# Making the rows of the maxima on ScalarE and GpSimd instead of VectorE in an attention block

## The reference, cut to what matters

```python
q, k, v = split(x @ W_qkv.T)            # 16 heads of 8
q, k = rope(q), rope(k)
scores = where(causal, q @ k.T / sqrt(8), -inf)
out = softmax(scores) @ v
x = layernorm(x + out @ W_o.T)
x = layernorm(x + x @ quantised(kernel) + bias + (x @ a) @ b)
```

## Time and profile before

| | |
|---|---|
| median of 3 runs | 443.64 us (441.98 to 443.79) |
| the profiled execution | 442.17 us, span 440.4 us |
| TensorE busy | 415.8 us, 94% |
| TensorE weight loads | 205.3 us, 47% |
| VectorE busy | 379.3 us, 86% |
| ScalarE busy | 317.4 us, 72% |
| GpSimd busy | 119.3 us, 27% |

### The profile page before, as it was taken

The page is one execution under the profiler, slowest core; times in us unless marked ns, Lnnn a source line. Parts: engine busy times, 40 slices in busy tenths (PEclk is TensorE's granted clock), DMA queues, the critical chain, the costliest instruction groups (busy, mean ns, idle before and its releaser), DMA issues.

```text
span 440.4 us, 8586 instructions
## 1 busy us (share of the span) xinstructions
PE 415.8 (94%) x3246; PEld 205.3 (47%) x3246; DVE 379.3 (86%) x491; ACT 317.4 (72%) x643; POOL 119.3 (27%) x188
## 2 busy tenths in 40 slices
PE   5989899799999999999999999999999999999982
PEld 2546445344436353455443644444354454435651
DVE  2878799899999999999999999999987988585585
ACT  2454884386975687777888788878788878898760
POOL 8979602102113100223110322011003012225463
PEclk9999999799999999999999999999999999999996
DMA  7522322210000000022200022200000000000001
GB/s 241 177 97 90 111 81 71 56 30 3 2 0 2 4 1 3 1 80 63 61 3 0 2 66 77 60 3 0 2 1 2 1 3 2 3 25 2 1 26 48
DMA packets 12201, 16.58 MB, mean 38 GB/s; under 512 B 2444, under 2 KB 7324, under 8 KB 12160
## 3 DMA queue, kind: packets, MB, share of 16 engines
q1 hardware_dynamic: 11072, 15.75, 11.3%
q0 software_dynamic: 1088, 0.28, 0.4%
HBM read 10.37 MB, written 5.24 MB: 35 GB/s over the span
## 4 chain that ended last, share of the span: by engine, by line
PE 81%; DVE 8%; ACT 5%; issue 3%; POOL 1%; DMA 1%; POOLq 0%; DVEq 0%; ACTq 0%
PE ps L1289 28%; PE ps L1275 23%; PE ps L1231 17%; DVE pmax L1052 7%; ACT probs L974 4%; PE ps L1199 3%; PE ps L1298 2%; PE ps L1245 1%; PE ps L1241 1%; PE ps L1205 1%; PE ps L1255 1%; PE ps L1317 1%; POOL rstd L856 1%; PE ps L1215 1%; DMA wqkv_sb<-in_L_attn_W_qkv_dram 1%
## 5 line engine op out<-in xcount | busy, mean ns | idle before, releaser
L1052 DVE TENSOR_REDUCE pmax<-ps 128x2 f32<-128x1024 f32 (+3 forms) x273 | 319.2, 1216 | 34.5 <-PE ps L1231 18.7
L974 ACT ACTIVATE probs<-ps 128x512 f32<-128x512 f32 (+2 forms) x576 | 285.4, 583 | 78.1 <-PE ps L1275 76.6
L1275 PE MATMUL ps<-qS,kS 64*128 64x512 f32 (+3 forms) x664 | 163.8, 404 | 2.7 <-DVE pmax L1052 1.3
L1231 PE MATMUL ps<-kS,qS 64*128 64x512 f32 (+3 forms) x640 | 141.9, 414 | 5.5 <-DVE pmax L1052 2.4
L1289 PE MATMUL ps<-probs,vP 128*9 128x512 f32 (+3 forms) x1328 | 144.3, 520 | 0.2
L1275 PEld LDWEIGHTS ps<-qS,kS 64*128 64x128 f32 x664 | 84.5, 186 | 85.5 <-ACT probs L974 61.4
L1231 PEld LDWEIGHTS ps<-kS,qS 64*128 64x128 f32 x640 | 67.1, 185 | 59.8 <-DVE pmax L1052 28.6
L881 POOL TENSOR_SCALAR_AFFINE_SELECT probs<-probs 128x512 f32<-128x512 f32 x64 | 40.3, 635 | 109.7 <-ACT probs L974 109.6
L890 POOL DMA_DIRECT2D qS<-mrows x34 | 19.6, 578 | 167.6 <-DVE mrows L1072 167.4
L1289 PEld LDWEIGHTS ps<-probs,vP 128*9 128x9 f32 x1328 | 22.2, 89 | 42.2 <-issue 24.4
L1245 PEld LDWEIGHTS ps<-causal_x,ident_x 64*128 64x128 f32 x188 | 19.1, 186 | 0.0
(11 more groups left out here) (116 smaller groups left out, 196.1 us busy)
## 6 DMA issues: line engine op xcount, KB each, us to landing
qS<-q_parts SPq DMA_DIRECT2D x52, 64.0 KB
kS<-k_parts SPq DMA_DIRECT2D x52, 64.0 KB
cs<-rope_tables_dram SPq DMA_DIRECT2D x4, 512.0 KB, 6.5
q_parts<-qp SPq DMA_DIRECT2D x4, 512.0 KB, 2.9
k_parts<-kp SPq DMA_DIRECT2D x4, 512.0 KB, 2.8
x_sb<-in_L_attn_x_dram SPq DMA_DIRECT2D x4, 256.0 KB, 5.7
out_dram<-rot SPq DMA_DIRECT2D x2, 256.0 KB, 2.3
qS<-mrows POOLq DMA_DIRECT2D x30, 8.0 KB, 1.8
```

The source lines that it names most:

```text
L974: nc.scalar.activation(probs[:, J % PRING, heads[0]:heads[-1] + 1:2, lo:hi], bank_of(("S", n, j, i))[:, 0:len(heads) * (hi - lo)].rearrang ...
L1052: nc.vector.tensor_reduce(dst, src, AX.X, ALU.max).then_inc(unit_free, 1)
L1231: last = nc.tensor.matmul(ps[:, HELD[e][hl], at:at + w], qS[rows, b, c, hp, ii * TOK:(ii + 1) * TOK], kS[rows, b, kk, hp, 0:w], start=i == ...
L1275: last = nc.tensor.matmul(bank_of(("S", n, j, i))[:, x * w:(x + 1) * w], kS[rows, b, j // TPC, hp, (j % TPC) * TOK:(j % TPC + 1) * TOK], q ...
```

## The change

ScalarE copies the transposed maxima as they are from the bank into a new buffer in SBUF, `mraw` (16 rows, 2 buffers of 256), and signals `rows_copied`, which now frees the bank. GpSimd waits for that, makes both parts out of `mraw` and then issues both DMAs as before, at the same place of its order. VectorE's function `rows` is gone. The planner's cost for `M` changes with it: 0.2 us on ScalarE, 0.6 us on GpSimd after a 0.2 us hand-over, nothing on VectorE, and `LANDING` counts from GpSimd. The whole order is planned again with that.

```diff
--- before.py
+++ after.py
@@ -353,8 +353,11 @@
                 self.give(self.act + self.TO_PE, self.sums)
                 self.due += ((self.act + self.TO_PE, "O", n),)
         elif kind == "M":
-            self.aside(0.25, 0.6, ready)
-            self.ready = self.ready[:e[0]] + (self.dve + self.LANDING,) + self.ready[e[0] + 1:]
+            self.act = max(self.act, self.whole(0.25, ready) + self.TO_ACT) + 0.2
+            self.side = (self.side[0] + 0.25, self.side[1])
+            self.give(self.act + self.TO_PE, self.took)
+            self.pool = max(self.pool, self.act + 0.2) + 0.6
+            self.ready = self.ready[:e[0]] + (self.pool + self.LANDING,) + self.ready[e[0] + 1:]
         elif kind == "O":
             g, c, first, end = TASKS[e[0]]
             self.aside(0.55 * (end - first) / TPC, 0.6, ready)
@@ -558,6 +561,7 @@
 
         pmax = sb("pmax", [128, 2, PAIRS, ALL_SLOTS])
         nmax = sb("nmax", [128, 2, 2 * PAIRS * TPC])
+        mraw = sb("mraw", [2 * PAIRS * TPC, 2, CH // 2])
         mrows = sb("mrows", [2 * PAIRS * TPC, 2, PARTS, CH // 2], fp32r)
         probs = sb("probs", [128, PRING, HG, CH])
 
@@ -607,6 +611,7 @@
         unit_free = sem("unit_free")
         nmax_done = sem("nmax_done")
         rows_done = sem("rows_done")
+        rows_copied = sem("rows_copied")
         turned_copied = sem("turned_copied")
         slots_set = sem("slots_set")
         s_done = sem("s_done")
@@ -666,7 +671,7 @@
             if copied_by_act(e):
                 RELEASE[e] = (turned_copied, 1 + sum(s is turned_copied for s, _ in RELEASE.values()))
             elif e[0] in RING_EVENTS:
-                RELEASE[e] = (rows_done, PARTS * (e[1] + 1)) if e[0] == "M" else (unit_free, 1 + sum(s is unit_free for s, _ in RELEASE.values()))
+                RELEASE[e] = (rows_copied, e[1] + 1) if e[0] == "M" else (unit_free, 1 + sum(s is unit_free for s, _ in RELEASE.values()))
             elif e[0] == "S":
                 RELEASE[e] = (exp_done, SET[e[1:]] + 1)
             elif e[0] == "PV":
@@ -884,6 +889,14 @@
             def load_maxima(n):
                 g, c, first, end = TASKS[n]
                 b, (lo, hi) = g % 2, queries(n)
+                count, w = rows_of(n)
+                src, to = mraw[0:count, n % 2, 0:w], mrows[0:count, n % 2, :, 0:w]
+                pool.wait_ge(rows_copied, n + 1)
+                if n >= 2:
+                    rows_in(pool, n - 2)
+                pool.tensor_copy(to[:, 0, :], src).then_inc(rows_done, 1)
+                pool.wait_ge(rows_done, PARTS * n + 1)
+                pool.tensor_tensor(to[:, 1, :], src, to[:, 0, :].bitcast(fp32), ALU.subtract).then_inc(rows_done, 1)
                 for a in range(PARTS):
                     pool.wait_ge(rows_done, PARTS * n + a + 1)
                     at, (count, w) = SHIFT_AT + a * SHIFT_STEP, rows_of(n)
@@ -982,12 +995,21 @@
                 lo, hi = queries(n)
                 nc.scalar.copy(oT[:, n % 2, lo:hi], bank_of(("PV", n, 0))[:, lo:hi]).then_inc(o_free, 1)
 
+            def copy_rows(n):
+                (count, w), e = rows_of(n), ("M", n)
+                act.wait_ge(unit_done, UNIT[e])
+                if n >= 2:
+                    act.wait_ge(rows_done, PARTS * (n - 1))
+                nc.scalar.copy(mraw[0:count, n % 2, 0:w], bank_of(e)[0:count, 0:w]).then_inc(rows_copied, 1)
+
             def copy_turned(n, k):
                 e, i, (lo, hi) = ("POST", n, k), turn(n)[0], queries(n)
                 act.wait_ge(unit_done, UNIT[e])
                 nc.scalar.copy((onT if k == 2 else x1T)[i][:, lo:hi], bank_of(e)[:, lo:hi]).then_inc(turned_copied, 1)
 
             for e in SCHEDULE:
+                if e[0] == "M":
+                    copy_rows(e[1])
                 if copied_by_act(e):
                     copy_turned(*e[1:])
                 if e == ("P", 0, 1):
@@ -1063,16 +1085,6 @@
                         nc.vector.tensor_reduce(to.rearrange("p (t h) -> p h t", t=2), of.rearrange("p l h (t k) -> p (l h) t k", t=2),
                                                 AX.X, ALU.max, negate=True).then_inc(nmax_done, 1)
 
-            def rows(n):
-                e, (count, w) = ("M", n), rows_of(n)
-                src, to = bank_of(e)[0:count, 0:w], mrows[0:count, n % 2, :, 0:w]
-                dve.wait_ge(unit_done, UNIT[e])
-                if n >= 2:
-                    rows_in(dve, n - 2)
-                nc.vector.tensor_copy(to[:, 0, :], src).then_inc(rows_done, 1)
-                dve.wait_ge(rows_done, PARTS * n + 1)
-                nc.vector.tensor_tensor(to[:, 1, :], src, to[:, 0, :].bitcast(fp32), ALU.subtract).then_inc(rows_done, 1)
-
             def quantise():
                 e = ("L",)
                 dve.wait_ge(wq_step, 6)
@@ -1154,8 +1166,6 @@
                     nc.vector.tensor_reduce(wst[:, 0:1], ffn_sb[:, :], AX.X, ALU.max, apply_absolute_value=True).then_inc(wq_step, 1)
                 if e[0] == "A":
                     row_max(*e[1:])
-                if e[0] == "M":
-                    rows(e[1])
                 if e[0] == "L":
                     quantise()
                 if e[0] == "O":
```

## The result

The changed kernel takes 449.26 us in the median of 4 runs (448.27 to 450.07), beside 443.01 for the kernel before in the same series: ratio 1.0142, 95% interval 1.0106 to 1.0177. It is 6.3 us slower. The forecast was 442.0 us and its range ended at 447.5.

A forecast was written before the change was run, and what follows sets the result against it. VectorE was taken to bind at the start, later coupled with TensorE. VectorE -3.1, ScalarE +0.5, GpSimd +0.7 and hand-over +0.3 sum to -1.6 us, so 442.0 us from a median of 443.64; range 436.5 to 447.5.

The forecast's parts named there:

- One reduce more or less on the chain is 1.2 us: Allowance for the newly planned order, whose fall the trace can't show: two reduces either way.
- a sum of -1.6: Whole kernel: the terms -3.1, +0.5, +0.7 and +0.3 us together, giving 442.0 us as the median.
- VectorE, -3.1 us: Pass A ends 9.0 us sooner without VectorE's rows; second-pass work moved there remains, so 9.0 x (1 - 0.652).
- the low end of 0.8: VectorE's gain if TensorE sets the end everywhere but the first stretch: 8.5% of 9.0 us.
- several us sooner: Sign expected in the profile after: the last unit of pass A several us sooner, and a fuller tail.
- ScalarE +0.5: 17 added copies out of a bank, 4.2 us in all, cost 0.2 to 4.2 us, nearer the low end.
- GpSimd +0.7: Two operations before the DMA issues, 0.76 us a task, delay selects or splits; 11/64 of at most 3.8 us.
- hand-over +0.3: From M's transpose to the first S: the planner places S 0.5 us later in five tasks, 0 to 2.6 us.
- the five: Tasks 0, 1, 4, 10, 16: GpSimd idle under 1 us before the issues; what follows is 0.76 us late.
- Too small a gain to count: Bank of M, freed after one ScalarE copy instead of two VectorE operations: no loss, and no gain counted.
- GpSimd's queue: Rival, chance 0.20: selects and splits behind the issues, and the first S behind the rows, wait; +3.8 us, 447.4 us.
- VectorE as the bound: Rival, chance 0.24: VectorE truly binds, so all 9.0 us and 0.8 come back less 1.5 costs; -8.3, 435.3 us.

The follow-up runs named there:

- x1: The changed kernel with the planner keeping its old cost for M, so in the order of the kernel before: ratio 1.0004, median 444.68 us.
- x3: The changed kernel with M's planned cost as its trace shows (0.25 us ScalarE, 0.1 hand-over, 0.76 GpSimd): 441.81 us, ratio 0.9958.
- x2: The kernel before, rows on VectorE, with the planner's new cost for M, so in the changed kernel's order: 457.36 us, ratio 1.0293.
- v1: The kernel before, rows on VectorE, with x3's planned cost, so in x3's order: 450.00 us, ratio 1.0140.
- p1: The changed kernel with x3's costs (0.75 instead of 0.76 on GpSimd) plus 1.15 us planned for both DMA issues: 445.32 us, ratio 1.0046.
- c4: The changed kernel with the planner's LANDING 4.1 and VectorE's idle-time weight 1.5: median 444.24 us, ratio 1.0014.
- b1: The kernel before with only the planner's LANDING at 3.5 instead of 4.0: median 448.27 us, ratio 1.0106.
- y1: The changed kernel with task 4's rows on GpSimd moved behind the last select of task 3: 448.93 us, ratio 1.0126.

## Why the prediction was wrong

The 6.3 us are 1.8 us of a later planned end and 4.5 us more of lag behind the plan. The step that failed is the last of the sum, "One reduce more or less on the chain is 1.2 us; I allow two of them either way": the new order was taken as a scatter of 2.4 us around a sum of -1.6. The runs show orders of the same instructions from 0.9958 to 1.0142, 8 us apart, and 1.0 to 1.0125 with the rows on VectorE. The scatter was larger than every term, and the kernel before stood at its favourable edge, which pushes a new draw upwards. I had its whole planner before me and priced the edit's load, not the draw: the plan alone would have shown the end 1.8 us later.

- **VectorE, -3.1 us.** In the old order no gain is left over after the costs (x1), which fits the low end of 0.8 better than the value taken; no run shows the gain by itself. In x3's order pass A runs ahead by 7.0 us at task 13, but the last `M`, and with it the end of pass A, by only 1.2 us, where the prediction wanted it several us sooner; in the changed kernel it came 9.4 us later. x3's whole is -1.9 us by ratio beside the -1.6 of the sum. That agreement is luck, one order out of many, and confirms no term.
- **ScalarE +0.5, GpSimd +0.7, hand-over +0.3.** Together with VectorE's part they come to 0 in x1, by an interval of 1.3 us down and 1.6 up. The first values began at 54.05 instead of 53.15, but the `M` of task 1 also came 0.9 later, so that shows nothing of the queue. The place that hurt was task 4, which I had named among the five; there 0.76 us was the wrong size, since in the new order all of its 2.1 us stand before a select. In the changed order the waits for selects are 8.6 us and the array's part 3.6, and the 0.7 is too small; in the old one they are 5.3 and 0.2.
- **The banks of M.** "Too small a gain to count" fits the old order, where x1 gains nothing. It left out that a new plan builds on the early release: an order made for it loses 7 to 8 us with the rows on VectorE (x2, v1), with 7.3 and 6.2 us of idle array at that bank.
- **The rivals.** GpSimd's queue had the sign and nearly the price (447.4), but x1 has all of its work and a loss of 0 by ratio and 1.3 us by the medians, so it isn't the cause by itself. It may have a share in the lag, at most the 4.5 us; p1, where it is planned for, has the least lag. VectorE as the bound, 435.3, with the Trainium skill's "Perfetto Trace Analysis", section "Identifying the Most-Contended Engine", behind it: in x1 the busiest engine after TensorE was relieved of 7.8 us and the time got no shorter.

What stays open: how the 4.5 us of lag divide. The lower clock lasted 6.9 us longer in the changed kernel's profile than in before's before 425 us. At half speed that is at most 3.4 us of lost work, and the table runs the same way (7.6 to 9.9 us of lag at 6.8, 10.1 to 13.5 above it). But no run set the clock alone, c4 and b1 have more of it at less lag, and one profile stands for many executions. The clock of each timed run says more. The kernel before, one program on three chips, has a median of 442.5 us in its 41 runs with a mean clock of 0.979 to 0.984, 445.1 in 8 runs at 0.972 and 447.8 in 8 at 0.961. The changed kernel's four runs are all at 0.972 or 0.973, 449.26 us. At the same clock it is therefore some 4 us slower, and about 2 of the 6.3 us go with the clock. x1, read in the same way, is 1.7 us slower (444.2 us in its 7 runs from 0.979 up, beside 442.5), so a part of the lag may be a cost of the move itself, though not the most of it.

## What to carry to other kernels

Where an order is searched from modelled costs, an edit is two changes: the work, and a new draw. Time the work in the old order and a few new orders at neighbouring settings before judging either; a kernel that stands at the best of its draws is likely to beat the first draw of a change. And an engine's cost in the model must hold all that its queue holds, DMA issues too, or the order puts what is urgent behind them.

The fastest here was x3, the changed kernel with its planned costs as measured: 0.9958 of before, 0.982 of the changed one.

## What the runs showed of the hardware that wasn't expected

- TensorE's granted clock fell to 1.2 GHz in the middle of the kernel in several orders, mostly near 51 us and near 150, for 3.4 or 6.8 us each. The array's busy time just before doesn't tell which: from 144 to 150 us it was 4.49 us in the changed kernel and 5.58 in y1, both with a fall at 150, and 5.04 in the kernel before, without one. In y1 the array had, by its modelled ends, no idle stretch above 0.4 us in the 20 us before that fall.
- The same work needn't show the same falls: y1 and the changed kernel are alike up to 140 us, and only y1 fell at 51.3. The 75 runs of the kernel before in the experiments had mean clocks from 0.961 to 0.984 and times from 448.3 to 442.1 us.
- GpSimd's subtraction of 16x128 took 449 ns beside VectorE's 278, its cast 280 beside 269: with one input the two engines are level at this size. GpSimd read SBUF there, and VectorE the bank.
